# Attention of a two-layer block: the denominator's matmuls in the same group as the values' matmuls, and reciprocals of a 128x16 tile filled by DMAs

## What is computed

```python
h = _sln(hidden, w, ln_g, ln_b, Wg, bg, Wb, bb)
qkv = (h @ Wqkv.T + bqkv).reshape(B, N, num_heads, hd, 3)
q = jnp.moveaxis(qkv[..., 0], 2, 1)
k = jnp.moveaxis(qkv[..., 1], 2, 1)
v = jnp.moveaxis(qkv[..., 2], 2, 1)
energy = jnp.einsum('bhqd,bhkd->bhqk', q, k)
att = jax.nn.softmax(energy, axis=-1) / D ** 0.5
out = jnp.einsum('bhqk,bhkd->bhqd', att, v)
out = jnp.moveaxis(out, 1, 2).reshape(B, N, D)
out = out @ Wp.T + bp
h1 = out + hidden
h2 = _sln(h1, w, ln_g, ln_b, Wg, bg, Wb, bb)
return h2 + h1
```

## Time and profile before

| | |
|---|---|
| median of three runs | 2079.34 us |
| span of the profiled execution | 2077.5 us |
| granted TensorE clock, mean of the span | 0.965 |
| TensorE busy | 1964.5 us (95%) |
| VectorE busy | 1383.0 us (67%) |
| GpSimd busy | 1105.7 us (53%) |
| ScalarE busy | 855.7 us (41%) |
| DMA read and written | 119.99 MB and 67.16 MB |

### The profile page before, as it was taken

How to read it: one execution, slowest core, us unless ns; L and a number is a source line. 1 busy time by engine, 2 the same in 40 slices (tenths; PEclk the granted TensorE clock), 3 DMA queues, 4 the chain that set the end, 5 groups by cost and what they waited for, 6 DMA issues and landing times. The chain is left out here.

```text
span 2077.5 us, 29213 instructions
## 1 busy us (share of the span) xinstructions
PE 1964.5 (95%) x9504; PEld 1203.7 (58%) x9504; DVE 1383.0 (67%) x1754; ACT 855.7 (41%) x1469; POOL 1105.7 (53%) x553
## 2 busy tenths in 40 slices
PE   6599999999998999989999999999999999998974
PEld 1488888888887888864444444444444444442652
DVE  3555665566455544447788778778777878876678
ACT  1323112311222222214666566656656666665212
POOL 0675556555652121223666666666665666665655
PEclk9799999999999999987999999999999999999987
DMA  7300101110125554664332133333213333021454
GB/s 238 111 31 22 51 30 40 30 50 20 31 102 183 177 187 177 207 186 93 77 82 49 41 83 77 82 83 74 51 47 83 77 83 83 11 83 59 139 166 147
DMA packets 104341, 189.24 MB, mean 91 GB/s; under 512 B 8186, under 2 KB 25722, under 8 KB 104220
## 3 DMA queue, kind: packets, MB, share of 16 engines
q1 hardware_dynamic: 85472, 176.71, 29.6%
q10 hardware_dynamic: 18560, 10.94, 1.8%
q0 software_dynamic: 192, 0.05, 0.0%
HBM read 119.99 MB, written 67.16 MB: 90 GB/s over the span
## 5 line engine op out<-in xcount | busy, mean ns | idle before, releaser
L1305 DVE TENSOR_REDUCE at_mrow<-banks 128x1 f32<-128x1024 f32 x512 | 614.7, 1222 | 198.1 <-PE banks L1133 198.1
L1389 POOL TENSOR_TENSOR at_pair<-at_probs 128x2048 f32<-128x2048 f32 x127 | 581.3, 4577 | 294.6 <-ACT at_probs L1278 294.6
L1278 ACT ACTIVATE at_probs<-banks 128x512 f32<-128x512 f32 x1024 | 556.9, 595 | 329.2 <-PE banks L1149 321.6
L1149 PE MATMUL banks<-early_qs,early_ks 98*128 98x512 f32 x1024 | 454.5, 447 | 11.3 <-issue 8.7
L1149 PEld LDWEIGHTS banks<-early_qs,early_ks 98*128 98x128 f32 x1024 | 193.0, 190 | 397.9 <-ACT at_probs L1278 350.5
L1133 PE MATMUL banks<-early_ks,early_qs 96*128 96x512 f32 x1024 | 399.0, 415 | 6.3 <-PEq L726 3.5
L1161 PE MATMUL banks<-at_probs,at_v 128*32 128x512 f32 x2048 | 276.2, 612 | 0.9 <-ACT at_probs L1278 0.9
L1133 PEld LDWEIGHTS banks<-early_ks,early_qs 96*128 96x128 f32 x1024 | 199.0, 197 | 46.4 <-DVE at_mrow L1305 19.5
L66 PE MATMUL banks<-l_ht,l_weights 128*128 128x512 f32 x768 | 178.8, 392 | 5.6 <-ACT l_gt L546 5.6
L66 PE MATMUL banks<-qk_nt,l_weights 128*128 128x512 f32 x768 | 177.1, 392 | 3.0 <-ACT qk_gt L861 3.0
L546 ACT ACTIVATE l_gt<-banks,mod 128x512 f32<-128x512 f32 x64 | 48.1, 777 | 313.9 <-PE banks L440 278.1
(11 more groups left out here) (124 smaller groups left out, 2069.4 us busy)
## 6 DMA issues: line engine op xcount, KB each, us to landing
qk_scratch<-qk_out SPq DMA_DIRECT2D x64, 512.0 KB, 2.9
early_ks<-qk_scratch SPq DMA_DIRECT2D x48, 512.0 KB, 6.7
early_qs<-qk_scratch SPq DMA_DIRECT2D x96, 256.0 KB, 11.3
v_scratch<-qk_v ACTq DMA_DIRECT2D x32, 256.0 KB, 2.4
at_v<-v_scratch SPq DMA_DIRECT2D x16, 512.0 KB, 14.9
attn_scratch<-at_out SPq DMA_DIRECT2D x32, 256.0 KB, 2.3
o_a<-attn_scratch SPq DMA_DIRECT2D x32, 256.0 KB, 6.4
o_x<-x_scratch SPq DMA_DIRECT2D x8, 1024.0 KB, 7.4
```

The lines of the kernel that those rows point to most:

```text
L1149: pe.matmul(et[j % 2][:], ks[0:98, slot, j, (i % KC) * P:(i % KC + 1) * P], qs[0:98, slot, i // KC, j, :], start=True, stop=True).then_inc ...
L1278: nc.scalar.activation(probs[:, i % 4, j, :], et[j % 2][:], ACT.Exp).then_inc(exp_done, 1)
L1305: nc.vector.tensor_reduce(mrow[:, half, u:u + 1], e_ps[u % 2], AX.XY, ALU.max).then_inc(max_done, 1)
L1389: nc.gpsimd.tensor_tensor(psum2[:, pair % 2], probs[:, a], probs[:, a + 1], ALU.add).then_inc(pair_ready, 1)
```

## The change

- The narrow products of a step stand in one group. den (now with a list of parts) does half of the 512 columns in each step, right behind av after the second head's energies, in place of all columns at the end of each second step. Pair p runs in steps 2p + 4 and 2p + 5. In steps 4 and 12 nothing, in steps 5 and 13 both parts of the first pair of a half. There are four heads x two parts per pair, so twice the number of records at half the width.
- The products for the maxima always stand in the same places: one ahead of the first head's energies, one ahead of the second's, one behind the third's and one behind the fourth's. turn_neg, take_neg and the negation come one step later, take_den one step later (3 and 11).
- For each half but the last: SP copies the four rows den_sb[0:P:HD] (one for each head) into den_c, 128 partitions x 16 (spread_den, 128 pieces of 64 bytes). VectorE takes the reciprocal of den_c into rden_c, at the end of step 5 (second half of the group before) and 13 (first half). SP stores rden_c to rden_scratch in HBM, waits until it has landed, and issues four loads, each of one head's 512 values to 32 partitions (widen_rden).
- GpSimd's finish waits for those loads and stands ahead of pairs 3 (second half of the group before) and 7 (first half). The last half takes its reciprocals from den_sb in one instruction.
- SP's order in a group: load_group, store of the group before's first half, spread of its second, place_neg, widen of that second half, store of that second half, spread of the first half, place_neg, widen of the first half.

```diff
-        TURN = (SWITCH + KC, SWITCH)
-        PIECES = KC
-        PC = CH // PIECES
+        TURN = (SWITCH + KC + 1, SWITCH + 1)
+        PARTS = 2
+        DC = CH // PARTS
+        DEN_STEP = KC // 2 - 1
+        ROWS = P // HG
+        DW = CH // ROWS
...
+        den_c = sb("at_den_c", [P, QH, DW])
+        rden_c = sb("at_rden_c", [P, QH, DW])
...
+            def spread_den(g, half):
+
+                sp.wait_ge(den_taken, halves(g, half))
+                if not (isinstance(g, int) and g == 0):
+                    sp.sem_inc(sh.sp_passed, 1)
+                    sp.wait_ge(rden_ready, halves(g, half) - 2)
+                sp.sem_inc(sh.sp_passed, 1)
+                sp.dma_start(den_c[:, half],
+                             den_sb[0:P:HD, half].rearrange("j (r c) -> j r c", c=DW)).then_inc(den_spread[half], 16)
+
+            def widen_rden(g, half):
+
+                first = isinstance(g, int) and g == 0
+                sp.wait_ge(rden_ready, halves(g, half))
+                if not first:
+                    sp.sem_inc(sh.sp_passed, 1)
+                    sp.wait_ge(rden_loaded[half], 16 * HG * g)
+                sp.sem_inc(sh.sp_passed, 1)
+                sp.dma_start(sh.rden_d[half].rearrange("j (r c) -> (j r) c", c=DW), rden_c[:, half]).then_inc(rden_stored[half], 16)
+                sp.wait_ge(rden_stored[half], 16 * (g + 1))
+                if not first:
+                    sp.sem_inc(sh.sp_passed, 1)
+                    sp.wait_ge(out_ready, halves(g, half) - 2)
+                sp.sem_inc(sh.sp_passed, 1)
+                for j in range(HG):
+                    sp.dma_start(rden[HD * j:HD * (j + 1), half],
+                                 sh.rden_d[half, j].partition_broadcast(HD)).then_inc(rden_loaded[half], 16)
+
...
+                if not first:
+                    store(g - 1, 0)
+                    spread_den(g - 1, 1)
                 place_neg(g, slot, 1)
                 if not first:
-                    store(g - 1, 0)
+                    widen_rden(g - 1, 1)
+                    store(g - 1, 1)
+                spread_den(g, 0)
                 if with_next:
                     place_neg(g + 1, (slot + 1) % RING, 0)
-                if not first:
-                    store(g - 1, 1)
-
+                widen_rden(g, 0)
...
-            def den(g, pair, turned=None):
+            def den(g, pair, parts, turned=None):
...
-                for j in range(HG):
-                    rows = slice(HD * j, HD * (j + 1))
-                    last = pe.matmul(den_ps[rows, :], ones_col[:], psum2[:, pair % 2, j, :],
-                                     start=n == 0, stop=n == KC // 2 - 1)
-                last.then_inc(den_done, 1)
+                for part in parts:
+                    cols = slice(DC * part, DC * (part + 1))
+                    for j in range(HG):
+                        last = pe.matmul(den_ps[HD * j:HD * (j + 1), cols], ones_col[:], psum2[:, pair % 2, j, cols],
+                                         start=n == 0 and part == 0, stop=n == KC // 2 - 1 and part == PARTS - 1)
+                    if part == PARTS - 1:
+                        last.then_inc(den_done, 1)
+
+            def den_of_step(g, i, with_next):
+
+                if i == KC // 2:
+                    return
+                if i == KC // 2 + 1:
+                    den(g, 0, range(PARTS), halves(g, 1))
+                elif i == KC + KC // 2 + 1:
+                    den(g, PAIRS // 2, range(PARTS), halves(g + 1, 0) if with_next else None)
+                elif i > KC // 2 and i != KC + KC // 2:
+                    den(g, (i - KC // 2) // 2, [i % 2])
...
                     for j in range(HG):
+                        if j < 2:
+                            for product in products[j:j + 1]:
+                                max_unit(*product)
                         energies(g, slot, i, j)
-                        for product in products[sum(behind[:j]):sum(behind[:j + 1])]:
-                            max_unit(*product)
+                        if j >= 2:
+                            for product in products[j:j + 1]:
+                                max_unit(*product)
                         if j == 1:
+
                             if i >= 1:
                                 av(g, slot, i - 1)
                             elif not first:
                                 av(g - 1, prev, STEPS - 1)
-
-                    if i % 2 == 0:
-                        if i >= 4:
-                            turned = {4: halves(g, 1), 12: halves(g + 1, 0) if with_next else None}.get(i)
-                            den(g, (i - 4) // 2, turned)
-                        elif not first:
-                            den(g - 1, PAIRS - 2 + i // 2)
+                            if i >= KC // 2:
+                                den_of_step(g, i, with_next)
+                            elif not first:
+                                den(g - 1, PAIRS - 2 + i // 2, [i % 2])
...
-                    if i == 2 and not first:
+                    if i == KC // 2 - 1 and not first:
                         take_den(g - 1, 1)
-                    if i == KC + 2:
+                    if i == KC + KC // 2 - 1:
                         take_den(g, 0)
...
-            def invert(g, half, piece):
-
-                if piece == 0:
-                    dve.wait_ge(den_taken, halves(g, half))
-                    if not (isinstance(g, int) and g == 0):
-
-                        dve.wait_ge(out_ready, halves(g, half) - 2)
-                cols = slice(piece * PC, (piece + 1) * PC)
-                nc.vector.reciprocal(rden[:, half, cols], den_sb[:, half, cols]).then_inc(rden_ready, 1)
+            def invert(g, half):
+
+                dve.wait_ge(den_spread[half], 16 * (g + 1))
+                if not (isinstance(g, int) and g == 0):
+                    dve.wait_ge(rden_stored[half], 16 * g)
+                nc.vector.reciprocal(rden_c[:, half], den_c[:, half]).then_inc(rden_ready, 1)
...
+                    if i == DEN_STEP + 2 and not first:
+                        invert(g - 1, 1)
+                    if i == KC + DEN_STEP + 2:
+                        invert(g, 0)
...
-                pool.wait_ge(rden_ready, PIECES * halves(g, half))
+                pool.wait_ge(rden_loaded[half], 16 * HG * (g + 1))
...
-                    if pair in (1, 5) and not first:
-                        finish(g - 1, pair // 4)
+                    if pair == 3 and not first:
+                        finish(g - 1, 1)
+                    if pair == PAIRS - 1:
+                        finish(g, 0)
```

More of the change, by code:

```diff
@@ L1027, in attention_stage @@
         den_done, den_taken = sem("at_den_done"), sem("at_den_taken")
+        den_spread = [sem(f"at_den_spread{i}") for i in range(QH)]
         rden_ready = sem("at_rden_ready")
+        rden_stored = [sem(f"at_rden_stored{i}") for i in range(QH)]
+        rden_loaded = [sem(f"at_rden_loaded{i}") for i in range(QH)]
         out_ready = sem("at_out_ready")
@@ L1192, in group @@
                     products = [(unit, keys) for unit in units_of_step(g, slot, i, with_next) for keys in range(2)]
-                    if i % 2 == 1:
-                        products += [(unit, 0) for unit in units_of_step(g, slot, i + 1, with_next)[0:1]]
-                        behind = (1, 1, 1, 2)
-                    elif first and i == 0:
-                        behind = (2, 0, 1, 1)
-                    else:
-                        products = products[1:]
-                        behind = (1, 0, 1, 1)
                     for j in range(HG):
+                        if j < 2:
+                            for product in products[j:j + 1]:
+                                max_unit(*product)
                         energies(g, slot, i, j)
-                        for product in products[sum(behind[:j]):sum(behind[:j + 1])]:
-                            max_unit(*product)
+                        if j >= 2:
+                            for product in products[j:j + 1]:
+                                max_unit(*product)
                         if j == 1:
@@ L1233, in _ @@
             av(G - 1, RING - 1, STEPS - 1)
-            den(G - 1, PAIRS - 2)
+            den(G - 1, PAIRS - 2, range(PARTS))
             for n in (2, 3):
@@ L1260, in take_den @@
                 if not (isinstance(g, int) and g == 0):
-                    act.wait_ge(rden_ready, PIECES * (halves(g, half) - 2))
+                    act.wait_ge(den_spread[half], 16 * g)
                 nc.scalar.copy(den_sb[:, half], den_ps[:]).then_inc(den_taken, 1)
@@ L1359, in _ @@
             groups(dve, group)
-            for piece in range(PIECES):
-                invert(G - 1, 1, piece)
-            dve.wait_ge(rden_ready, PIECES * halves(G - 1, 1))
+            dve.wait_ge(den_taken, halves(G - 1, 1))
+            dve.wait_ge(out_ready, halves(G - 1, 1) - 2)
+            nc.vector.reciprocal(rden[:, 1], den_sb[:, 1]).then_inc(rden_ready, 1)
```

(4 more changed lines are left out.)

10 lines of the change are left out of this document (1 added, 9 removed).

## The result

The changed kernel takes 2224.45 us, the median of four runs (2218.65 to 2226.01), against 2079.0 for the kernel before, run four times beside it (2077.96 to 2079.47). The ratio is 1.069, with a 95% interval of 1.067 to 1.072. The forecast was 2048, in a range of 2041 to 2076: the change was expected to make the kernel faster and made it slower, and the time lies far outside the range.

A forecast was written before the change was run, and what follows sets the result against it. TensorE, busy 95% of the span, was taken as the bound. From the profiled 2077.5 us: -37 for denominator groups, +4 for group 15, 1.8 from span to median, 1.7 for frictions, giving 2048, range 2041 to 2076.

The forecast's parts named there:

- Left alone: Parts counted as unchanged, including turn_neg and its negation moving one step later in the attention stage; no cost given.
- One narrow group per step: Attention stage: denominators join av's narrow group, half-width rounds cost 0.215 us, steps 3.53; saves 0.31 us per two steps.
- -33 was forecast for the stage: Attention stage's net: 37 us less from 120 denominator groups, 4 us more in group 15.
- Rival 1: Half-width products: weight loads or dispatch, not columns, set their pace, giving 2154 or 2185 us; chance 0.12 for both.
- the +48 behind 2096: TensorE time if eight more records a step cost 25 ns each: 48 us in 240 steps.
- the +137 behind 2185: TensorE time if a small fixed cost for eight new records added 0.54 us a step: 137 us in 253 steps.
- The small frictions: Allowance of 1.7 us for 500 more rounds on TensorE, 3 ns each.
- Rival 2: DMA chain of the reciprocals late by 1 us beyond slack: 2063 in one half, 2079 in both; chance 0.15.
- the signs I named: VectorE idle before the reciprocal, GpSimd before at_out: waits over 1 us, followed by ScalarE or TensorE waits.
- Reciprocals off VectorE: 256 pieces of 0.54 us (136.8 us) leave VectorE, 31 small ones come; worth nothing on the path.
- Group 15, +4 us: Last group: nothing covers TensorE's wait for exponentials after merging, two steps take 7.04 against 6.41 us, in 6 pairs.
- Slower: Chance 0.14 of a slower kernel: 0.12 from dearer narrow pieces, 0.02 from a late DMA chain.

The follow-up runs named there:

- the shifted kernel before: The kernel before with only the transposition and negation of the maxima one key step later (transposition ahead of that step's denominators): 2234.57 us, 1.075 of before.
- the full-width kernel: The changed kernel with the negation one step earlier and full-width denominators every second step in place of half-width ones in each: 2053.71 us, 0.988 of before.

## Why the prediction was wrong, step by step

- *The step that failed: "Left alone. ... turn_neg moves one step later, together with its negation."* I put it at nothing, without a reason and without a row. The distance between the two stayed the same. What changed was the distance to something I didn't look at: GpSimd's sum. The shift put the negation from 3.8 us behind a sum's start (1107.27, 1111.10) to 0.7 behind it (1102.90, 1103.59). What the runs showed in its place: the negation is held until the sum ends, 3.89 us in the median, TensorE waits for it 30 times, and the clock falls at each of these places. Price: 179.4 us, by the two spans; the forecast missed the result by 176.5.
- *What in the trace of before would have shown it.* The negations there:

```profile
L1312 DVE TENSOR_SCALAR at_neg<-at_mrow x32: 174/784/791, 938.8 to 1865.9; 128x16 fp32r<-128x16 f32 x32
```

  The minimum is 174 ns and the median 784, for one shape. The longer ones all end 0.03 to 0.04 us behind the end of a sum. A bound for the moved step could have been had from it, as an estimate: the negation starts 3.83 us behind a sum's start; one new step later, at 3.83 + 3.53 = 7.36, it lies 0.3 us behind the start of the next sum, which comes after 7.06. Held to that one's end it would take 4.58 - 0.3 = 4.3 us, more than the 3.53 us of one step. In the changed kernel it was 3.9, in the shifted kernel before 4.3.
- *One narrow group per step, 3.53 us, rounds of 0.215:* right, to the hundredth, in the changed kernel and in the one with the negation earlier. The sum came out nearly: -33 was forecast for the stage, and from the first values' product to the last denominators it is 35.9 us shorter there (954.8, 918.9). An ordinary group gained 2.4 us (forecast 8 x 0.31 = 2.5), the three groups with a loop's end 10.8 together in place of 7, and 2.7 us were lost outside the stage. That the span is 2044.3, and the forecast's 2044.5, is thus luck in part.
- *Rival 1, dearer narrow pieces:* refuted by the full-width kernel, 7.06 us for two steps either way. The 60 cycles a matmul that the Trainium skill gives (TensorEngine Tiling, Instruction Overhead) don't show here at half width in the narrow form. Two sums of this rival were also counted wrong: the change adds 1016 records (9504 to 10520), four a step and not eight, so what I added for each new record comes out twice too large (the +48 behind 2096 would be 24, the +137 behind 2185 some 68). The small frictions, too, were taken for 500 more rounds, and there are 254.
- *Rival 2, the DMA chain late:* the signs I named came, without a price. GpSimd waited for the DMA before the multiplication and VectorE hardly at all:

```profile
POOL at_out L1415 <- DMA at_rden<-rden_scratch: 45.9, 24, 3.2
...
  DMA at_den_c<-at_den_sb: 4.6, 2
```

  The 45.9 us in 24 waits only replace a wait: in the kernel before GpSimd waited 46.9 us at 24 places for VectorE's reciprocals. They fall into its slack, and the version without the DMAs is as fast (0.983 of before, both). Costed at zero, and zero it was. The bound I gave for "slower", over 2.1 us late in both halves, doesn't follow from 31 us for one microsecond: that is level with before already.
- *Reciprocals off VectorE, worth nothing:* right by the same pair.
- *Group 15, +4 us:* right: 48.2 us before, 52.6 merged, 48.6 apart again.
- *The clock.* I allowed 3 us "whether it does so once more or less". It did so 30 times more, at each wait of TensorE for the negation, and cost 66.7 us.
- *The chances.* "Slower" had 0.14, all of it on mechanisms that turned out to cost nothing. The one that decided had none. That the time went the way of those 0.14 bears none of them out.

What stays open: why the clock stays low longer at the loop ends of the full-width version, and how the 112.7 us divide between the wait itself and the reductions behind it (TensorE's rows show 69.0 and 28.8 us for these in the changed kernel, 97.8 together, of which 7.4 stand in the kernel with the negation earlier too; the rest isn't attributed). The runs show which forms are held and until when; what in the chip holds them, no run shows. Not tried: the negation from PSUM or on another engine.

## What to carry to other kernels

When a step is moved in time, check it against the instructions of every engine that run beside it at its new place, not only against the queues it passes: here the multiplication by a scalar and the instructions with two SBUF inputs that landed inside a GpSimd sum lasted until it ended, however small they were, while a reduction and a reciprocal didn't. Look for it in the trace before: one shape whose minimum and median durations differ several times, and whose ends coincide with those of GpSimd's instructions. And price a stop of TensorE twice, once for its length and what is late behind it, and once for the low clock that may follow, here 3.8 and 2.3 us a place.

## What the runs showed of the hardware that I had not expected

- How small an instruction can be and still be held: a TENSOR_SCALAR of 128x16, 0.17 us on its own, took 4.35 us at the longest in the shifted kernel before. A TENSOR_REDUCE of that size (0.159 us) and a RECIPROCAL (0.24 for 128x16, 0.54 for 128x64) weren't held.
- Two such instructions in a row wait twice where GpSimd's work comes in short pieces (0.65 and 1.14 us in the mean, with the sum in four), so short pieces gained less than their length promised.
- A stop of 2.24 us, with one of 0.87 behind it, was followed by a granted clock of 0.52 in a busy stretch, and the clock fell at each of the 30 such places. With the 2.24 us filled by useless products, and the 0.87 left, the clock stayed at 1.00 there, and the stage had 0.99.
